# Feed-forward products 15 periods behind a tile's projections, from its stored transposed form, and their weight prepared in the first periods of the loop

## The reference

```python
w = simulate_quantize_int4(kernel)     # scale = max|kernel| / 7, round, clip to -8..7
ffn = xn @ w + bias + (xn @ a) @ b     # a: 512x16, b: 16x512
q, k, v = heads(xn @ Wq.T), heads(xn @ Wk.T), heads(xn @ Wv.T)
diff_sq = |q|^2 + |k|^2 - 2 q.k
distance = arccosh(1 + 2 diff_sq / ((1 - |q|^2) (1 - |k|^2)))
attn = softmax(-distance) @ v @ Wo.T
out = x + attn + ffn
```

## Time and profile before

| | us |
|---|---|
| median of 3 runs | 2388.22 (2387.29 to 2389.18) |
| the profiled execution | 2385.05 |
| its span, first to last instruction | 2383.4 |
| TensorE busy in it | 2267.3 |
| VectorE busy | 2055.4 |
| ScalarE busy | 2109.4 |
| GpSimd busy | 257.4 |

### The profile page before, as it was taken

One profiled execution on the slowest core, in us unless ns is written; L12 is line 12 of the kernel. 1 busy time (PEld: TensorE's weight loads), 2 busy tenths in 40 slices (PEclk: granted clock), 3 DMA queues, 4 the chain that ended last, 5 costly groups with the idle time before them and its releaser, 6 DMA issues.

```text
span 2383.4 us, 44990 instructions
## 1 busy us (share of the span) xinstructions
PE 2267.3 (95%) x17416; PEld 812.0 (34%) x17416; DVE 2055.4 (86%) x2748; ACT 2109.4 (89%) x1939; POOL 257.4 (11%) x193
## 2 busy tenths in 40 slices
PE   6999999999999999999999999999999999987777
PEld 2433333333333333333333333333333333322222
DVE  7779888899988889998889998888998988876676
ACT  4379999999999999999999999999999999999994
POOL 0111110111011111011011101111101101100012
PEclk9999999999999999999999999999999999999998
DMA  4453333543545443354525344453344454243433
GB/s 156 124 138 90 110 97 103 140 109 103 138 132 143 115 121 110 116 146 129 134 84 145 105 139 132 130 140 104 115 114 146 128 138 106 83 133 90 115 97 86
DMA packets 355424, 285.00 MB, mean 120 GB/s; under 512 B 81132, under 2 KB 294252, under 8 KB 355208
## 3 DMA queue, kind: packets, MB, share of 16 engines
q1 hardware_dynamic: 355208, 282.10, 42.6%
HBM read 159.77 MB, written 121.36 MB: 118 GB/s over the span
## 4 chain that ended last, share of the span: by engine, by line
PE 56%; DVE 19%; ACT 13%; issue 10%; DMA 2%; SPq 0%; ACTq 0%; POOL 0%; DVEq 0%; POOLq 0%
PE pM L286 20%; PE pU L206 12%; PE pO L218 12%; PE pZ L234 6%; DVE root L816 6%; ACT root L506 6%; ACT root L502 6%; DVE root L821 3%; DVE stats L649 1%; DVE al L766 1%; DVE shares L764 1%; PE pM L276 1%; PE pM L259 1%; DVE ah L765 1%; DVE f_o L756 1%
## 5 line engine op out<-in xcount | busy, mean ns | idle before, releaser
L502 ACT ACTIVATE root<-pU 128x1024 f32<-128x1024 f32 x1024 | 1033.1, 1030 | 70.4 <-PE pU L206 66.3
L506 ACT ACTIVATE root<-root 128x2048 f32<-128x2048 f32 x512 | 983.3, 1921 | 89.4 <-DVE root L816 88.7
L816 DVE TENSOR_SCALAR root<-root 128x2048 f32<-128x2048 f32 x512 | 670.2, 1309 | 80.1 <-ACT root L502 78.1
L206 PE MATMUL pU<-QS,KS 100*128 100x512 f16 x2048 | 616.2, 383 | 68.2 <-ACT root L502 59.0
L821 DVE TENSOR_TENSOR root<-root 128x2048 f32<-128x2048 f32 x256 | 589.5, 2303 | 43.7 <-PE pO L218 28.4
L218 PE MATMUL pO<-root,VX 128*32 128x512 f32 x4096 | 548.4, 605 | 7.2 <-ACT o_s L512 7.0
L206 PEld LDWEIGHTS pU<-QS,KS 100*128 100x128 f16 x2048 | 143.6, 98 | 608.1 <-issue 281.8
L234 PE MATMUL pZ<-root,ones 128*32 128x512 f32 x2048 | 271.5, 599 | 4.2 <-DVE root L821 4.2
L964 POOL TENSOR_TENSOR sqr<-qk 128x512 f32<-128x512 f32 x112 | 151.9, 1356 | 1058.3 <-ACT qk L527 914.8
L286 PE MATMUL pM<-Wqh,xT 128*128 128x512 f16 x480 | 162.8, 383 | 2.3 <-DVE f_o L756 1.5
L286 PE MATMUL pM<-Wvh,xT 128*128 128x512 f16 x480 | 161.9, 379 | 0.5 <-DVE Wvl L628 0.5
(11 more groups left out here) (224 smaller groups left out, 2144.0 us busy)
## 6 DMA issues: line engine op xcount, KB each, us to landing
v_d<-v_o SPq DMA_DIRECT2D x64, 264.0 KB, 2.1
k_d<-kx SPq DMA_DIRECT2D x64, 264.0 KB, 2.1
KT<-k_d SPq DMA_DIRECT2D x64, 264.0 KB
VX<-v_d SPq DMA_DIRECT2D x64, 264.0 KB
xts<-in_x SPq DMA_DIRECT2D x32, 512.0 KB, 4.1
res_d<-f_o SPq DMA_DIRECT2D x64, 256.0 KB, 3.9
QS<-qh_d SPq DMA_DIRECT2D x128, 128.0 KB
KS<-kh_d SPq DMA_DIRECT2D x128, 128.0 KB
```

What stands on the lines that cost most here:

```text
L206: mm = pe.matmul(pU[:, col:col + HALF], KS[i][:, h, j * P:(j + 1) * P], QS[i][:, h, half * HALF:(half + 1) * HALF], start=True, stop=True)
L502: act.activation(root[:, q % RING, cols], pU[:, cols], ACT.Square).then_inc(squared, 1)
L506: act.activation(root[:, q % RING, :], root[:, q % RING, :], ACT.Sqrt).then_inc(rooted, 1)
L816: v.tensor_scalar(root[:, q % RING, :], root[:, q % RING, :], CS * CS, CS * CS, ALU.max, ALU.subtract).then_inc(clamped, 1)
```

## The change

- The feed-forward product of tiles 0 to 55 moves to period m + 7 (`F_LAG` = 7, so m = p - 7), on the same steps 12 to 14; that of tiles 56 to 63 goes to steps 1 to 3 of period m. The prologue has none.
- Its operand is no longer kept: every tile's transposed, split form is stored in `xT_d` (`store_xT`, at step 7) and loaded again (`load_feed`, at step 2, or for the last eight tiles at step 5 of the period before and at step 1 of period 56), with the tile's rows of x beside it (`xr`). `xT` has two buffers instead of three, `xt` two instead of three.
- GpSimd adds the bias to `xr`, without the wait for the feature transpose. `take_f` writes into `xr` in place, and this stays on chip for `take_o` of the next period, so `load_res` and `load_res_last` are gone. `take_o` writes to a buffer of its own.
- The feed-forward weight is loaded into `shares` and prepared in periods 0 to 4; Wo follows into the same buffer and is prepared in periods 4 to 6.
- In the prologue the products have fixed banks: q 0, k 1, v 4, transposes 5, 2 and 3.
- Loads of x wait until both tiles in the buffer are normalised, not only for their variance.

```diff
+F_LAG = LEAD - 1
...
+            def feed(m, b, first, last):
+                late = m >= NT - LEAD
+                t = xT[m % 2] if late else fT[m % 2]
+                if first == 0 and late:
+                    pe.wait_ge(fT_late[m % 2], ((m - NT + LEAD) // 2 + 1) * 16)
+                elif first == 0:
+                    pe.wait_ge(fT_loaded[m % 2], (m // 2 + 1) * 16)
...
+                mm = product(pM[b], lambda c: t[:, 0, c, :], lambda c: t[:, 1, c, :], W["f"], first, last)
...
             def behind(p, k):
-                n, o, even = p + LEAD, p - LEAD, p % 2 == 0
+                n, m, o, even = p + LEAD, p - F_LAG, p - LEAD, p % 2 == 0
...
+                elif k in (1, 2, 3):
+                    if k == 1 and even:
+                        pe.wait_ge(taken["o"], o)
+                        pe.wait_ge(feat_split[1], NT)
+                    elif k == 1:
+                        pe.wait_ge(taken["f"], f_place[m - 1] + 1)
+                    feed(p, 0, 4 * k - 4, 4 * k)
+                if k == 7 and p in (1, 2):
+                    pe.wait_ge(x_split, n + 2)
+                    low_rank_rows(2 * p - 2, 0)
...
+                    if k == 12 and p in (1, 2):
+                        low_rank_rows(2 * p - 1, 0 if even else 1)
...
+                if 0 <= m < NT - LEAD:
+                    if even and k in (12, 13):
+                        feed(m, 0, 6 * k - 72, 6 * k - 66)
+                    elif not even and k in (12, 13, 14):
+                        feed(m, 1, 4 * k - 48, 4 * k - 44)
...
             for n in range(LEAD):
...
+                project(n, "k", 1, 0, 12)
+                transpose_x(n + 1, 5)
...
+                project(n, "v", 4, 0, 12)
+                if n:
                     pe.wait_ge(feat_split[0], n)
+                transpose_feat(n, 0, 2)
+                if n:
+                    pe.wait_ge(feat_split[1], n)
+                transpose_feat(n, 1, 3)
...
@@ ScalarE @@
             def behind(p, k):
-                if p == 2 and k == 8:
+                if p == 3 and k == 12:
+                    high(4, "f", 3)
+                if p == 5 and k == 12:
                     high(3, "o", 4)
...
@@ VectorE @@
             def behind(p, k):
+                if p == 0:
+                    if k == 1:
+                        v.wait_ge(w_loaded["f"], 16)
+                        largest_of("f", 5, "raw")
+                    elif k == 9:
+                        quantise(0)
+                    elif k == 14:
+                        quantise(1)
+                if p == 1:
+                    if k == 1:
+                        quantise(2)
+                    elif k == 10:
+                        fold(0, 0)
+                if p == 2:
+                    if k == 0:
+                        fold(1, 1)
+                    elif k == 9:
+                        fold(2, 0)
+                    elif k == 14:
+                        fold(3, 0)
+                if p == 3 and k == 1:
+                    v.wait_ge(folded, KC)
+                    largest_of("f", 4, "f")
+                if p == 3 and k == 9:
+                    scale_of(4, 5, W_TOP)
+                if p == 4 and k == 1:
+                    low(4, "f", 3)
+                if p == 4 and k == 14:
+                    v.wait_ge(w_loaded["o"], 16)
+                    largest_of("o", 3, "o")
+                if p == 5 and k == 9:
                     scale_of(3, 6, W_TOP)
...
+                if p == 6 and k == 1:
                     low(3, "o", 4)
...
+                if k == 0 and even and 1 <= m < NT - LEAD:
+                    take_f(m - 1, 1)
+                if k == 4 and n >= NT:
+                    take_f(p, 0)
...
+                if k == 14 and even and 0 <= m < NT - LEAD:
+                    take_f(m, 0)
...
@@ GpSimd @@
             for n in range(LEAD, NT):
                 square_qk(n, 0)
                 square_qk(n, 1)
...
+                if n >= LEAD + F_LAG:
+                    add_bias(n - LEAD - F_LAG)
...
@@ SyncE @@
+            def load_feed(m):
+                rows, i = slice(m * P, (m + 1) * P), m % 2
+                if m < NT - LEAD:
...
+                    sy.dma_start(fT[i][:, :, :, :].rearrange("p s c n -> p (s c n)"), xT_d[rows, :]).then_inc(fT_loaded[i], 16)
...
+                    sy.dma_start(xr[:, i, :], x[rows, :]).then_inc(xr_loaded[i], 16)
+                else:
+                    for parity in range(2):
+                        sy.wait_ge(xT_stored[parity], NT // 2 * 16)
+                    sy.wait_ge(made["v"], NT)
...
+                    sy.dma_start(xT[i][:, :, :, :].rearrange("p s c n -> p (s c n)"), xT_d[rows, :]).then_inc(fT_late[i], 16)
...
             def behind(p, k):
                 if k == 1 and p and p % 8 == 0:
                     all_stored(min(n, NT))
                     load_stack(p // 2, 1)
-                if k == 2 and o >= 0:
-                    load_res(o)
+                if k == 2 and 0 <= m < NT - LEAD:
+                    load_feed(m)
+                if n == NT and k == 1:
+                    load_feed(p)
+                if n >= NT and k == 5 and p + 1 < PERIODS:
+                    load_feed(p + 1)
...
+                if n + 1 < NT and k == 7:
+                    store_xT(n + 1)
```

More of the change, by code:

```diff
@@ L108, in fast @@
         root = sb("root", [P, RING, G4 * HALF])
-        xts = sb("xts", [P, 6, DM])
-        xt = [xts[:, 2 * i:2 * i + 2, :] for i in range(3)]
+        xts = sb("xts", [P, 4, DM])
+        xt = [xts[:, 2 * i:2 * i + 2, :] for i in range(2)]
         xn = sb("xn", [P, DM])
-        xT = [sb(f"xT{i}", [P, 2, KC, P], F16) for i in range(3)]
+        xT = [sb(f"xT{i}", [P, 2, KC, P], F16) for i in range(2)]
+        fT = [sb(f"fT{i}", [P, 2, KC, P], F16) for i in range(2)]
         qk, kx = sb("qk", [P, 2, DM]), sb("kx", [P, KC, KW])
@@ L293, in project, with low_rank_rows @@
                     mm.then_inc(made[k], 1)
+            def feed(m, b, first, last):
[5 more added lines that the diff above has]
+                    pe.wait_ge(fT_loaded[m % 2], (m // 2 + 1) * 16)
+                if m == 0 and first == 0:
+                    pe.wait_ge(w_low, 4)
+                mm = product(pM[b], lambda c: t[:, 0, c, :], lambda c: t[:, 1, c, :], W["f"], first, last)
+                if last == 3 * KC:
+                    mm.then_inc(made["f"], 1)
+            def low_rank_rows(c, b):
+                if c == 0:
+                    pe.wait_ge(rank_loaded, 2 * 16)
+                pe.matmul(pM[b][:, :], At[:, c * P:(c + 1) * P], Bl, start=True, stop=True).then_inc(low_rank, 1)
             def output(o, b, first, last):
@@ L396, in behind @@
                         transpose_feat(n, 1, 0)
[L399 to L403, removed]
+                if n >= NT and k == 12:
+                    if even:
+                        pe.wait_ge(taken["o"], o + 1)
+                    else:
+                        pe.wait_ge(kv_taken, (p + 1) // 2)
+                if 0 <= m < NT - LEAD:
[3 more added lines that the diff above has]
+                        feed(m, 1, 4 * k - 48, 4 * k - 44)
+                if n < NT and even and k == 14:
+                    pe.wait_ge(kv_taken, p // 2 + 1)
+                    transpose_feat(n, 1, 1)
+            pe.wait_ge(small_loaded, 16)
+            transpose_x(0, 5)
             for n in range(LEAD):
-                u = 7 * n
                 pe.wait_ge(x_split, n + 1)
@@ L809, in take_o @@
                 v.wait_ge(made["o"], o + 1)
-                v.wait_ge(res_loaded[o % 2], (o // 2 + 1) * 16)
-                t = res_i[:, o % 2, :]
-                v.scalar_tensor_tensor(out=t, in0=pM[b][:, :], scalar=scale[:, IVO:IVO + 1], in1=t, op0=ALU.mult, op1=ALU.add).then_inc(taken["o"], 1)
+                v.wait_ge(taken["f"], f_place[o] + 1)
+                if o >= 2:
+                    v.wait_ge(out_stored[o % 2], o // 2 * 16)
+                v.scalar_tensor_tensor(out=out_o[:, o % 2, :], in0=pM[b][:, :], scalar=scale[:, IVO:IVO + 1], in1=xr[:, o % 2, :],
+                                       op0=ALU.mult, op1=ALU.add).then_inc(taken["o"], 1)
             def clamp(q):
@@ L878, in behind @@
                         moments((n + 3) // 2)
-                    if k == 14 and even:
-                        take_f(n, 0)
+                if k == 14 and even and 0 <= m < NT - LEAD:
+                    take_f(m, 0)
             dve.up(v.memset(ones[:, :], V_SCALE))
@@ L990, in gpsimd_program @@
             everywhere(scale[:, 2:3], 2, largest["v"])
-            everywhere(top[:, 6:7], 5, largest["f"])
-            everywhere(scale[:, 4:5], 4, summed_w["f"])
-            g.wait_ge(bias_loaded, 16)
-            for n in range(LEAD):
-                add_bias(n)
             for n in range(LEAD, NT):
@@ L1064, in store_aug, with store_f @@
+            def store_f(m):
+                t = res_last[m - NT + LEAD] if m >= NT - LEAD else xr[:, m % 2, :]
+                sy.wait_ge(taken["f"], f_place[m] + 1)
```

(1 more changed line is left out.)

369 lines of the change are left out of this document (172 added, 197 removed).

## The result

The changed kernel takes 2399.28 us (median of 5 runs, 2391.86 to 2402.99), the kernel before 2388.22: a ratio of 1.0045, 95% interval 1.0034 to 1.0055. A second series gave 2398.49 against 2389.27, 1.0037 (1.0023 to 1.0050). The profiled execution was the fastest of the first series (2391.86, span 2390.2).

| stage | before | after | difference | forecast |
|---|---|---|---|---|
| prologue, to the first square | 136.8 | 109.2 | -27.6 | -27.3 |
| first square to the copy in period 7 | 251.5 | 245.8 | -5.7 | +0.6 |
| period 7 to 55 | 1688.9 | 1706.1 | +17.2 | +1 |
| 55 to 56 | 32.5 | 45.7 | +13.2 | +7.5 |
| 56 to 63 | 215.7 | 226.9 | +11.2 | +6 |

A forecast was written before the change was run, and what follows sets the result against it. Bound by TensorE in prologue and middle, by mutual waits of TensorE and ScalarE in periods 1 to 7, by ScalarE at the end. Terms -27.3 -6.7 +7.3 +1 +7.5 +6 = -12.2: span 2371.2, median 2376.0, range 2364 to 2385.

The forecast's parts named there:

- -27.3 forecast: Prologue: without the fourth product tiles take 10.2 us, first square at 109.5 instead of 136.81; bounds -24 and -29.
- the forecast gave back 1.2 us: Prologue start: of some 3.5 us lost at the lower clock behind a wait, a shorter gap returns 1.2.
- such a loss is mostly absorbed: +1: Middle periods: GpSimd's bias, now right behind the second square, may lengthen VectorE's clamp; +1 us, bounds -2 and +10.
- rival C: Middle: bias meets VectorE's clamp in all 49 periods, 0.85 us each, full price 41, about 2416 us; chance 0.06.
- The rule cited from the Trainium skill: VectorE's two-port forms and GpSimd share a pair of ports as an exclusive lock; the other fully blocks.
- the traffic that I had as nothing: Middle: three new DMA issues a period, one less, and 0.5 MB more, all costed at nothing.
- +7.5 with a bound of +9: Period 56: first late load, queued behind the last batch's stack, lands about 2111 and delays distances; +7.5 us, bounds +4, +9.
- +6 forecast: Periods 56 to 63: two products beside ScalarE come in bursts, 1.3 an even and 0.35 an odd period; bounds +2, +12.
- +0.6 forecast in all: First square to period 7: product removed from periods 0 to 6, -6.7 us, and weight prepared there, +7.3.
- The price of 1.1 for a low half: Weight preparation: a 2.3 us VectorE piece cost 1.1 for Wo's low half; two searches and one low half, +3.3.
- the 0.95 taken: Periods 0 to 6: gain per period from removing the feed-forward product, between 0.65 and 1.8; times 7, -6.7 us.
- 1.2 was taken: Weight preparation: three VectorE level passes of some 1.3 us, put in gaps, at 0.4 each.

The follow-up runs named there:

- experiment 1: Changed kernel with GpSimd's bias add waiting for q's feature transpose again, as before the change: 2387.49 us, 1.0003 to the kernel before.
- experiment 2: Kernel before the change with only the bias add's wait for the feature transpose taken out: 2402.17 us, 1.0064.
- experiment 7: The version with both mended, loading only 16 of 128 rows of the transposed form and x for tiles 2 to 55: 2371.02 us, 0.9929.
- experiment 3: Changed kernel with tile 56's load of transposed form and x rows moved from step 1 of period 56 to step 5 of period 55: 2387.01 us, 1.0002.
- experiment 5: The version with both mended, second product of periods 56 to 63 spread over steps 0 to 5, two matmuls each, take and store two steps later: 2370.26 us.
- the version with both mended: Changed kernel with the edits of experiment 1 and experiment 3 together (bias late, first late load early): 2373.49 us, 0.9951 to the kernel before.
- experiment 6: The version with both mended, doing only one of 12 matmuls of the feed-forward product of tiles 56 to 63: 2376.25 us, 0.9948.

## Why the prediction was wrong

*Prologue: right*, path and size. -27.3 forecast, -27.6 found; tiles come at the latency of the norm chain, two in 21.0 us, as the forecast had it (the keys come evenly, every 10.5). That it is so near is in part luck: of the low clock at the start the forecast gave back 1.2 us, in this trace it is gone altogether (granted clock 1.00 from 25 to 45 us, 0.91 before the change), and in the second one it is there as before, with a first square at 111.0.

*Middle: the step that turned the sign.* "With TensorE full and VectorE at 90%, such a loss is mostly absorbed: +1". It wasn't: +17.2, of which 12.5 stand in the even periods; experiment 1 gives 12.1 of them back, and experiment 2 makes 16.0 in the kernel before by the bias alone. This is my rival C, given 0.06. Its mechanism was right and its price too high: 0.85 was taken for all 49 periods; it is 1.05 on the clamp in even periods, 0.69 at the period's end, and nothing in odd ones. The argument against it was a clamp of 2.07 us inside a window in which TensorE stays full. That clamp is of an even period too (26), and what comes behind it was not read: ScalarE's root waited 1.38 us for it.

```profile
1053.11 1.91 ACT L506 ACTIVATE root<-root 128x2048 f32<-128x2048 f32 x1 [1.38 <-DVE root L816]
```

Such a clamp stands in every period of the middle, before and after, so whatever it costs was in the 34.88 already, and no run takes it out. I read a full TensorE at one place as the slack of the stage. The rule cited from the Trainium skill (SBUF — State Buffer, Who interferes with whom) holds in these rows: the clamp of 2.27 ends 1.1 us after the bias does, about its usual length. The other 4.7 of the +17.2 are the round trip of z, delayed by the traffic that I had as nothing (experiment 7).

*Period 56: right cause, wrong size.* +7.5 with a bound of +9, found 13.2 (12 by experiment 3). The load was issued 0.6 us behind the stack, as forecast, and landed 4.9 us after its issue where I had 3.4. What the forecast left out is the clock: it fell 2.1 us into TensorE's wait of 9.58 and stayed at the lower level until 6.1 us after its end. ScalarE gets its next square only after a third of a product, a value sum and a sum of ones at that pace: 12.99 of wait on ScalarE for 9.58 on TensorE.

*Last periods: +6 forecast, +11.2 found*, inside the bounds. Bursts were most of the reason (experiment 5). An even late period costs 1.6 where the clock doesn't fall and 3.2 where it does (32.3 and 33.9 instead of 30.7), and I had 1.3; an odd one costs 1.2 (31.4 instead of 30.2), and I had 0.35.

*Periods 0 to 6: too dear.* +0.6 forecast in all, -5.7 found. The folds and searches of VectorE in periods 1 to 6 cost nothing, since with the product gone ScalarE binds and VectorE has time. The price of 1.1 for a low half was misread: it is the bias that blocked VectorE in that very period (experiment 2), the same collision as in the middle, and three pieces were priced by it. A high half, with the low half behind it, cost 1.6 to 1.9, as said. The product's removal gave 0.75 in an even period (34.2 to 33.45), less than the 0.95 taken. The level passes cost 1.5 to 3.9, where 1.2 was taken.

The errors of opposite signs don't cancel: -6 here, +16, +6 and +5 there, and -1.6 at the end. They make 2390.2 of the 2371.2 for the span. The median then lies 9 us above that span, since this execution was the fastest of its series; 4.8 had been added for it, and in the second series it is 2.6.

## What to carry to other kernels

When an operation on GpSimd is freed of a wait, look up what VectorE runs in that very place, for each parity of the loop; a busy share of 90% is no cover when the step behind it is on the path. A load that moves to the boundary of a stage has to be issued before the burst that feeds the next stage, since the queue is in program order. A round trip through memory has to be followed to the store's landing, not only to the load's. And work put beside a full ScalarE should be spread a little over each step, not placed in a few.

## What the runs showed that I had not expected

The clock falls in well filled periods too. In the version with both mended it fell in three of the four even late periods, for 3.4 us each. Each time TensorE had stood idle for 1.86 us, waiting for ScalarE's square:

```profile
2110.06 0.60 PE L221 MATMUL pU<-QS,KS 100*128 100x512 f16 x2 [1.86 <-ACT root L544]
```

These periods were 33.9 us against 32.3 in the fourth, where it didn't fall: 1.6 us for a fall. The idle time alone doesn't decide: all four have the same 1.86, and in the changed kernel's first trace the clock fell behind two of four. With two matmuls a step (experiment 5) this gap is gone and the clock didn't fall in any late period; in the other versions with two a step it fell in these periods only behind gaps of 3.3 us and more, which have other causes (experiment 5). And taking work away from TensorE made nothing faster (experiment 6).

The bias on GpSimd and a small operation of VectorE collide as well as the large ones: 128x32 took 1.29 us instead of 0.19, and the whole period 1.1 more.
